# Two expert stages with their tokens sorted by expert on the chip, in units of 128 rows

## The reference, cut to what matters

```python
logits = x @ router.T (+ router_b)          # 8 experts
p = softmax(logits); top_p, top_i = top_k(p, 2)
h = gelu(x @ w1[e].T + b1[e])               # 128 -> 512, e in top_i
y = h @ w2[e].T + b2[e]                     # 512 -> 128
out = sum(top_p * y)                        # block 2: weights scaled to sum 1, and a shared expert for all tokens added
```

## Time and profile before

| | us |
|---|---|
| median of 3 runs (4932.38 to 4941.92) | 4935.69 |
| the profiled execution | 4945.66 |
| its span, first to last instruction | 4943.9 |
| PE busy in it | 3746.8 (76%) |
| DVE, ACT, POOL busy in it | 2553.2, 2187.2, 1043.4 |
| mean granted clock of TensorE | 0.851 of full speed |

### The profile page before, as it was taken

How to read it: one execution, slowest core, us unless ns; L and a number is a source line. 1 busy time by engine, 2 the same in 40 slices (tenths; PEclk the granted TensorE clock), 3 DMA queues, 4 the chain that set the end, 5 groups by cost and what they waited for, 6 DMA issues and landing times. The chain is left out here.

```text
span 4943.9 us, 64940 instructions
## 1 busy us (share of the span) xinstructions
PE 3746.8 (76%) x19738; PEld 2542.2 (51%) x19800; DVE 2553.2 (52%) x6640; ACT 2187.2 (44%) x4248; POOL 1043.4 (21%) x1066
## 2 busy tenths in 40 slices
...
GB/s 37 67 65 5 9 69 26 39 0 0 0 11 10 18 1 1 0 18 1 1 0 16 1 0 0 0 0 34 1 0 0 5 0 0 0 2 0 18 0 17
DMA packets 45621, 58.54 MB, mean 12 GB/s; under 512 B 14058, under 2 KB 37836, under 8 KB 44588
## 3 DMA queue, kind: packets, MB, share of 16 engines
...
## 5 line engine op out<-in xcount | busy, mean ns | idle before, releaser
L418 PEld LDWEIGHTS bank<-moe_w,moe_hidden 128*128 128x128 f32 x5376 | 626.6, 192 | 78.7 <-issue 76.8
L418 PE MATMUL bank<-moe_w,moe_hidden 128*128 128x128 f32 x5376 | 630.3, 275 | 0.0
L408 PE MATMUL bank<-normed_t,moe_w 128*128 (+1 forms) x1344 | 615.6, 600 | 11.5 <-ACT moe_hidden L470 8.2
L470 ACT ACTIVATE moe_hidden<-bank,moe_b 128x512 f32<-128x512 f32 x544 | 372.8, 687 | 505.8 <-PE bank L408 504.3
L546 DVE SCALAR_TENSOR_TENSOR branch<-bank,moe_weights,branch 128x128 f32<-128x128 f32 x768 | 216.3, 345 | 707.8 <-PE bank L418 703.9
L90 POOL TENSOR_TENSOR branch_norm_shifted<-branch_norm_moments,eps 128x4 f32<-128x4 f32 x64 | 12.7, 198 | 1889.8 <-DVE branch_norm_moments L83 1889.8
L408 PEld LDWEIGHTS bank<-normed_t,moe_w 128*128 128x128 f32 x1344 | 244.9, 193 | 256.0 <-issue 240.0
L1987 POOL TENSOR_TENSOR local_size<-local_size,local_half_powers 128x8 f32<-128x8 f32 x128 | 257.0, 2008 | 203.3 <-DVE local_size L2053 199.2
L1691 PE MATMUL bank<-local_wqkv,local_shifted 128*128 128x512 f32 x384 | 211.2, 644 | 57.0 <-DVEq L2045 24.0
L1496 DVE TENSOR_TENSOR ssm_mixer<-ssm_decay,bank 128x384 f32<-128x384 f32 x256 | 133.2, 552 | 202.8 <-PE bank L1158 179.5
L1308 ACT ACTIVATE ssm_decay<-bank 128x384 f32<-128x384 f32 x256 | 120.3, 489 | 192.4 <-PE bank L1131 147.4
...
## 6 DMA issues: line engine op xcount, KB each, us to landing
rwkv_kept<-rwkv_keep SPq DMA_DIRECT2D x8, 768.0 KB, 11.8
...
moe_w<-in_moe_w_dram SPq DMA_DIRECT2D x2, 2048.0 KB
...
```

Source lines behind the costliest of these rows:

```text
L408: pe.matmul(hbank[n % 4][:], w1[:, e, f * P:(f + 1) * P], source_t[:, bass.ds(i * PN, PN)], start=True, stop=True).then_inc(hidden_up, 1)
L418: last = pe.matmul(obank[e % 2][:, t * P:(t + 1) * P], hid[:, e % 2, f, t * P:(t + 1) * P], w2[:, e, f, :], start=(f == 0), stop=(f == chu ...
L470: act.activation(hid[:, e % 2, f, :], hbank[n % 4][:], ACT.Gelu_apprx_tanh, bias=b1[:, n:n + 1] if bias else 0.0).then_inc(hidden_done, 1)
```

## The change

A new function `sorted_moe` takes the place of `moe_block` for `moe0` and `moe2`. It computes a picked expert's rows only.

- The logits come straight from `normed_t` as weights: one matmul of eight columns for each tile, and one addition or copy on DVE for all. `moe_block`, which stays for `moe3`, gets the same logits; it no longer waits for the expert weights ahead of them.
- DVE finds both picks as masks, PE counts (a matmul with ones and one with a triangle of ones), and fourteen more DVE instructions turn the counts into a row number (slot) for each of a token's two picks. The tokens are handled in two halves of 16 tiles. In each half an expert's rows start at a multiple of 128; 40 units of 128 rows hold them whatever the gate says.
- POOL scatters the rows of `normed` to DRAM by slot, one transfer for each tile and pick (64 in all, 32 a half). For `moe0` SP first writes zeros over that DRAM (ten stores of 512 KB).
- For each of the 80 units: SP loads 128 rows, PE transposes them, ACT copies them to `rows_t`, DVE reads the unit's expert number into a register and copies that expert's record (both weight matrices and biases, 1156 numbers a partition) to one of four buffers, PE multiplies up and ACT applies Gelu, PE multiplies down, DVE adds the bias, SP stores 128 rows to DRAM.
- POOL gathers a pair's rows by slot (16 tiles' picks are 32 transfers for four pairs), DVE weighs and adds both picks of a token (`mix`), and the tail follows. The pairs of the first half are mixed in groups 6 to 9 of ten (eight units are a group), those of the second half behind the last unit.
- `moe0`'s shared expert is computed for all pairs ahead of the units, beside the sort.
- `Tail` of the stages ahead of both (`rwkv`, `ssm`) now keeps rows.

PE before: the body of `moe0` for one pair, from the loop's start (names as in the code, without numbers).

The diff, cut to its core:

```diff
--- before.py
+++ after.py
...
         @block.tensor
         def _(pe):
+            pe.wait_ge(router_in, 16 * router_loads)
+            for t in range(TILES):
+                last = pe.matmul(small[:, t * EXPERTS:(t + 1) * EXPERTS], source_t[:, t * P:(t + 1) * P], router[:],
+                                 start=True, stop=True)
+            last.then_inc(logits_up, 1)
...
-                    pe.wait_ge(logits_down, m * 2)
-                    for t in range(PT):
-                        last = pe.matmul(obank[k][:, t * EXPERTS:(t + 1) * EXPERTS],
-                                         logit_rows[:, k, t * P:(t + 1) * P],
-                                         core.ident[0:EXPERTS, 0:EXPERTS], start=True, stop=True)
-                    last.then_inc(logits_up, 1)
...
+UNIT = P
+HALVES = 2
+HALF_TILES = TILES // HALVES
+UNITS = HALF_TILES * 2 + 8
+GROUP = 8
...
+            if shared:
+                sp.wait_ge(blank_ready, 1)
+                for h in range(HALVES):
+                    for g in range(GROUPS_PER_HALF):
+                        sp.dma_start(core.rows_dram[h][g * GROUP * P:(g + 1) * GROUP * P, :].rearrange(
+                            "(k p) c -> p k c", p=P), blank).then_inc(blanked, 16)
+            sp.dma_start(records[:], dram[f"{name}_records"]).then_inc(records_in, 16)
...
+                wait_from(sp, rows_turned, n - GROUP + 1)
+                sp.dma_start(rows_in[:, k, :], core.rows_dram[h][bass.ds(row, P), :]).then_inc(rows_loaded[k], 16)
...
+            def store(h, g, k):
+                n = g * GROUP + k
+                row = (n - h * UNITS) * P
+                sp.wait_ge(out_ready, n + 1)
+                sp.dma_start(core.outs_dram[h][bass.ds(row, P), :], outs[:, k % 4, :]).then_inc(outs_stored[k % 4], 16)
...
+                for k in range(GROUP):
+                    if h + 1 < HALVES and k == 2:
+                        sp.wait_ge(sorted_in[h + 1], 16 * 2 * HALF_TILES)
+                    if k < 2 or h + 1 < HALVES:
+                        load(h + (k >= 2), final_group, k + 6)
+                    store(h, final_group, k)
...
+            def ranks():
+                pe.wait_ge(tables_in, 16)
+                pe.wait_ge(picks_ready, 1)
+                flat = picked[:].rearrange("p t e -> p (t e)")
+                pe.matmul(rbank[:, 0:TILES * EXPERTS], tables[:, ONES:ONES + P], flat, start=True, stop=True)
+                pe.matmul(lbank[:, 0:TILES * EXPERTS], tables[:, EARLIER:EARLIER + P], flat, start=True,
+                          stop=True).then_inc(ranks_up, 1)
...
+            def turn(g, k):
+                g, k = g + k // GROUP, k % GROUP
+                n = g * GROUP + k
+                pe.wait_ge(rows_loaded[k], (g + 1) * 16)
+
+                wait_from(pe, rows_taken, n - 1)
+                pe.transpose(tbank[k % 2][:, 0:UNIT], rows_in[:, k, :], core.ident[:]).then_inc(rows_turned, 1)
+
+            def up(g, k):
+                n = g * GROUP + k
+                pe.wait_ge(rows_taken, n + 1)
+                pe.wait_ge(record_ready, n + 1)
+
+                wait_from(pe, hid_done, n - 1)
+                for f in range(CH):
+                    last = pe.matmul(hbank[k % 2][:, f * UNIT:(f + 1) * UNIT], record[:, k % 4, f * P:(f + 1) * P],
+                                     rows_t[:, k % 2, :], start=True, stop=True)
+                last.then_inc(up_done, 1)
+
+            def down(g, k):
+                g, k = (g, k) if k >= 0 else (g - 1, GROUP - 1)
+                n = g * GROUP + k
+                pe.wait_ge(hid_done, n + 1)
+
+                wait_from(pe, out_ready, n - 1)
+                for f in range(CH):
+                    last = pe.matmul(obank[k % 2][:, 0:C], hid[:, k % 2, f, :],
+                                     record[:, k % 4, W2 + f * P:W2 + (f + 1) * P], start=(f == 0), stop=(f == CH - 1))
+                last.then_inc(down_done, 1)
+
+            def slot(g, k, low=0):
+                final = low == ALL_GROUPS
+                if not (final and k == GROUP - 1):
+                    turn(g, k + 1)
...
+                if not (low == 0 and k == 0):
+                    down(g, k - 1)
...
+                act.activation(rows_t[:, k % 2, :], tbank[k % 2][:, 0:UNIT], ACT.Identity).then_inc(rows_taken, 1)
+
+            def slot(g, k, low=0):
+                n = g * GROUP + k
+                final = low == ALL_GROUPS
+                if not (final and k == GROUP - 1):
+                    take_rows(g, k + 1)
+                act.wait_ge(up_done, n + 1)
+
+                wait_from(act, down_done, n - 1)
+                for f in range(CH):
+                    last = act.activation(hid[:, k % 2, f, :], hbank[k % 2][:, f * UNIT:(f + 1) * UNIT],
+                                          ACT.Gelu_apprx_tanh, bias=record[:, k % 4, B1 + f:B1 + f + 1])
+                last.then_inc(hid_done, 1)
+                if tail.turned and k == 1 and low >= GROUPS_PER_HALF + 2:
...
+            pool.wait_ge(slots_ready, 1)
+            if shared:
+                pool.wait_ge(blanked, 16 * ALL_GROUPS)
+            for t in range(TILES):
+                for k in range(2):
+                    pool.indirect_dma_start(core.rows_dram[t // HALF_TILES][:, :], bass.IndirectOffsetOnAxis(ap=slots[:, k, t:t + 1], axis=0),
+                                            core.normed[:, t, :], None).then_inc(sorted_in[t // HALF_TILES], 16)
+
+            def gather(i):
+                for t in range(i * PT, (i + 1) * PT):
+                    for k in range(2):
+                        pool.indirect_dma_start(found[:, k, t, :], None, core.outs_dram[t // HALF_TILES][:, :],
+                                                bass.IndirectOffsetOnAxis(ap=slots[:, k, t:t + 1], axis=0)
+                                                ).then_inc(found_in[i], 16)
+
+            per_half = PAIRS // HALVES
+            for h in range(HALVES):
+                for b in range(4):
+                    pool.wait_ge(outs_stored[b], 16 * (h + 1) * UNITS // 4)
+                for i in range(h * per_half, (h + 1) * per_half):
+                    gather(i)
+                    if i > h * per_half:
+                        tail.pool(pool, i - 1)
+                tail.pool(pool, (h + 1) * per_half - 1)
+
...
+            each = [P, HE, UNITS]
+            steps = tables[:, STEPS:STEPS + UNITS]
+            dve.scalar_tensor_tensor(wide[:], steps.unsqueeze(1).broadcast_to(each), float(UNIT),
+                                     many[:].unsqueeze(2).broadcast_to(each), ALU.mult, ALU.is_lt)
+            dve.drain()
...
+            flat_both = lambda buffer: buffer[:].rearrange("p k t e -> p k (t e)")
+            by_pick = lambda buffer: buffer[:].rearrange("p k t e -> p (k t) e")
...
+            def fetch(g, k):
+                g, k = g + k // GROUP, k % GROUP
+                n = g * GROUP + k
+                expert = dve.value_load(table[0:1, bass.ds(n, 1)], min_val=0, max_val=EXPERTS - 1)
+
+                wait_from(dve, down_done, n - 3)
+                dve.tensor_copy(record[:, k % 4, :], records[:, bass.ds(expert, 1), :].rearrange(
+                    "p e r -> p (e r)")).then_inc(record_ready, 1)
+
+            def mix(i):
+                dve.wait_ge(found_in[i], 16 * 2 * PT)
...
+                                             share_of[:, 1, i * PT + t:i * PT + t + 1], core.branch[:, t, :],
+                                             ALU.mult, ALU.add)
+                dve.drain()
+                tail.dve_branch(dve, i)
+
+            def slot(g, k, low=0):
...
+                n = g * GROUP + k
+                final = low == ALL_GROUPS
+                if not (final and k + 2 >= GROUP):
+                    fetch(g, k + 2)
+                dve.wait_ge(down_done, n + 1)
+                if not (low == 0 and k < 4):
+                    dve.wait_ge(outs_stored[k % 4], (g * 2 + k // 4) * 16)
+                dve.tensor_tensor(outs[:, k % 4, :], obank[k % 2][:, 0:C], record[:, k % 4, B2:B2 + C],
+                                  ALU.add).then_inc(out_ready, 1)
+                dve.drain()
+
+            fetch(0, 0)
+            fetch(0, 1)
+            groups(dve, slot, ((1, GROUPS_PER_HALF + 1),))
+            for g in range(GROUPS_PER_HALF + 1, ALL_GROUPS):
+                i = g - GROUPS_PER_HALF - 1
+                for k in range(GROUP):
+                    slot(g, k, ALL_GROUPS if g == ALL_GROUPS - 1 else g)
+                    if k == 0:
+                        mix(i)
+                    if k == 3:
+                        tail.dve_stream(dve, i)
+                    if k == 6:
+                        tail.dve_fresh(dve, i)
+            for i in range(PAIRS // 2, PAIRS):
+                mix(i)
...
         if "rwkv" in blocks:
-            rwkv_block(core, Tail(core, "rwkv", keep_rows=False, turned=True), dram["x"])
+            rwkv_block(core, Tail(core, "rwkv", keep_rows=True, turned=True), dram["x"])
             core.end_of_block()
```

(5 more changed lines are left out.)

368 lines of the change are left out of this document (324 added, 44 removed).

## The result

| | us | ratio to before, 95% |
|---|---|---|
| before, in the group of the record | 4936.88 (4932.38 to 4941.92, 4 runs) | |
| changed, on record | 4755.36 (4754.10 to 4758.67, 4 runs) | 0.9633, 0.9616 to 0.965 |
| forecast | 4560 (4450 to 4765) | 0.924 |
| changed again (e9, 2 runs) | 4618.37 | 0.9348, 0.9321 to 0.9375 |
| changed again (e16b, 4 runs) | 4613.50 | 0.9335, 0.9319 to 0.935 |

The kernel is faster, by 182 us where 376 were forecast.

A forecast was written before the change was run, and what follows sets the result against it. PE bound both expert bodies; afterwards DVE was to pace units at 2.25 us. Stages of 369 and 364 us (-216, -149) and -11 in the third gave -376: 4570, or 4560 us on the median's scale, range 4450 to 4765.

The forecast's parts named there:

- The shared expert ends on PE at 14.2 + 60 = 74: First stage's preparation: shared expert at 7.5 us a pair hides the scatter; table load and records follow, first unit at 81.
- C: Dear transfers by row number on POOL: c = 2.2 us each, +151, 4711 us; chance 0.15.
- F: Slower: POOL becomes the bound; with c = 4.5 a stage takes 647 us, in all +184, 5120 us; chance 0.05.
- G: DVE's record copies hold up POOL's transfers, c 1.85 while units run, 9 us a stage: 4578 us; chance 0.04.
- D: A unit's steps don't overlap, since the register read waits until DVE is empty: 3.5 us a unit, +200, 4760; chance 0.12.
- E: TensorE clock granted at 1.2 GHz in the units: 3.86 us a unit on PE, +190, 4750 us; chance 0.06.
- issue price c: POOL's time to issue one scatter or gather by row number: 1.2 us, the middle of 0.33 and 2.2.
- the register read: DVE reading a unit's expert number from SBUF into a register: 1.0 us, the middle of 0.07 and 1.8.
- A: The main case: DVE sets the unit's pace at 2.25 us against PE's 1.93 and ACT's 1.78; 4560 us, chance 0.38.
- B: Cheap register reads at 0.07 us: DVE 1.32 a unit, PE binds at 1.93, 45 less a stage, 4470; chance 0.18.
- PE's busy time: Sign of the forecast: PE busy near 210 us in the first sorted stage and 150 in the second.
- Behind the last unit: Stage ends: POOL's 32 x 1.2 issues, landing, waits and last mix take 73 us, 77 in the second stage.

The follow-up runs named there:

- e9: The changed kernel itself, unaltered, run once more in a later group on chip 4: 4618.37 us (2 runs).
- e16b: The changed kernel itself, unaltered, run beside e15b on chip 2: 4613.50 us (4 runs).
- e7: Changed kernel without the register read: DVE copies the record of expert k for a group's k-th unit, so units meet the wrong expert: 4574.65 us.
- e15b: e13 plus second half's scatter and first half's gathers spread over units, first-stage scatter spaced by small powers, epsilon added by DVE: 4599.81 us (4 runs).
- e11: Changed kernel with the shared expert's pairs 2 to 7 in a loop on PE and ACT, the same file as e4 run again: 4611.30 us.
- e13: Changed kernel with shared expert's bias in DVE's addition, its pairs in loops, POOL's powers between gathers, one register read for two units: 4700.25 us (4 runs).
- e2: Changed kernel with the scatters of both stages replaced by as many plain 64 KB transfers from POOL, rows in order: 4631.65 us.
- e14: Changed kernel with second half's scatter and first half's gathers spread, one behind each of 32 units, and POOL's powers between these gathers: 4647.57 us (2 runs).
- e4: Changed kernel with the shared expert's pairs 2 to 7 in a loop of two pairs on PE and ACT: 4750.86 us.

## Why the forecast was wrong, step by step

**The step that failed** is "The shared expert ends on PE at 14.2 + 60 = 74 ... up to c = 1.3 the scatter costs nothing here", and its twin, units beside transfers at 2.25. On record the shared expert ended at 165.3, and 16 gathers stretched their group from 17 to 34.6 us. What I had wrong is that an engine which issues transfers costs only its own time. Rivals C and F priced POOL's time, G what DVE's copies do to POOL; none had PE, ACT and DVE losing 1.1 us a transfer. It is worth 95 + 48 = 143 us of the 195 by which the result missed (137 to 142 by the medians), and it was absent in four of seven groups of runs, where the miss is 55.

Three things were luck. 4755 lies inside 4450 to 4765, but the upper bound stood for D and E, at 4760 and 4750, and neither came true. The issue price c and the register read, 1.2 and 1.0, were middles between rows of other kinds. Measured are 1.27 (0.96 busy and 0.30 between), and for the read some 0.8: the gap ahead of a record copy is 0.98 in the mean with it and 0.16 without it, in e7.

**The rest, against e16b.** First stage 401.7 for 369, second 378.7 for 364, third 274.9 for 270.7.
- First unit: PE's first matmul of one at 101.6 us (972.38) for 81. The logits were right (13.8 for 12), the sort and gate ready at 39 for 34, hidden. The shared expert was mis-sized: I charged 7.5 us a pair with its bias matmuls, it takes 9.4.

```profile
940.50 3.60 PE L693 MATMUL bank<-normed_t,moe_own 128*128 128x512 f32 x8
944.03 0.48 PE L702 MATMUL bank<-moe_own,ones_row 1*128 1x128 f32 x2
944.45 1.16 PE L704 MATMUL bank<-moe_own,moe_found 128*128 128x128 f32 x8
```

  A bias product with one row takes 0.41 (944.03 to 944.45), a full one of 128 columns 0.27 (four in some 1.09, to the next bias). Four of the first are 1.65 a pair where I had charged 0.49, and sixteen of the second 4.4 where rows 3 gave 3.57: over eight pairs 16 of the 20.6 us. Both come with the one-row products: in e15b, without them, 32 full ones take 7.31 us, 0.23 each, and the shared expert ends at 75.2, where I had 74; with its loop alone (e11) it ends at 94.8.
- Second stage's first unit at 77.4 for 72: slots at 31.8 for 29, 32 issues in 40.8 for 38.
- Units: 218 and 217 us from the first matmul to the last addition, for 214. A unit 2.13 (forecast 2.25), a group with a pair 27.8 and 27.3 (26.4). The gap ahead of the record copy is 0.91 to 1.27 (1.0 taken, and 0.15 for drains), the copy 0.76 (0.80), the addition 0.29 (0.30), in e16b's timeline:

```profile
1060.42 0.29 DVE L1008 TENSOR_TENSOR moe_outs<-bank,moe_record 128x128 f32<-128x128 f32 x1 [0.35 <-PE bank L748]
1061.98 0.76 DVE L979 COPY moe_record<-moe_records 128x1156 f32 x1 [1.27 <-issue]
1062.66 0.28 DVE L1008 TENSOR_TENSOR moe_outs<-bank,moe_record 128x128 f32<-128x128 f32 x1
```

  So A's account of the unit stands, and e7 shows both its halves: without the read 1.90, for 1.93. The rival B's 0.07 is out, D too. The floor of about 600 ns for a tensor_load in the Trainium skill ("DMA: Bandwidth & Descriptors", "Latency and other measured facts") is below these gaps, which contain the read and a drain, and below the some 0.8 of the read alone.
- PE's busy time, a sign of the forecast at near 210 and 150, was 279 and 195 in e16b. In the first stage the shared expert with its ranks is 79 of it, for 60, the first 48 units are 104, for 93 at 1.93 each, and the other 32, at a clock of 0.85, 78, for 62.
- Behind the last unit: 82 and 84, for 74 and 78 with the barrier's 1.4. Most of what is missing is a drain of POOL between two small operations, where gathers stand just ahead of them. In e16b's timeline:

```profile
1231.39 0.21 POOL L92 TENSOR_TENSOR branch_norm_shifted<-branch_norm_moments,eps 128x4 f32<-128x4 f32 x1
1233.37 1.04 POOL L94 TENSOR_TENSOR branch_norm_rstd<-branch_norm_shifted,minus_half 128x4 f32<-128x4 f32 x1 [1.77 <-issue]
...
1237.80 0.20 POOL L92 TENSOR_TENSOR x_norm_shifted<-x_norm_moments,eps 128x4 f32<-128x4 f32 x1 [3.40 <-DVE x_norm_moments L85]
1238.15 1.01 POOL L94 TENSOR_TENSOR x_norm_rstd<-x_norm_shifted,minus_half 128x4 f32<-128x4 f32 x1
```

  1.77 us behind gathers, 0.15 where none came since the last drain. Three pairs have it once. A pair takes 17.9 us (1204.80 to 1222.68), and I had 8 x 1.2 + 6 = 15.6. e13 keeps the drains and ends at 77 in both stages, e15b has none and ends at 70 and 74. Transfers in flight can't be all of it: on record the first such gap of a stage's units is 6.71 us, at 1172.6, 18 us behind the last gather, where e16b's gathers land in 2.5. What the drain waits for is open.
- Third stage: its 64 matmuls took 13.8, at the lower clock (0.50 granted), for 12, and the gain was 6.9 for 11.

**The other rivals.** E: no unit took the 3.86 us of the lower clock. Over the first 40 units it is 0.98 and 0.97 in the two stages of e16b, in groups 6 to 9 0.85 and 0.86; whether that has a part in the 0.9 to 1.4 us that a group takes over the forecast is not separated. In the held-up stretch on record it is 0.89 in 911 to 938, where PE begins to starve at 928, and 0.50 behind it. G: sixteen gathers beside record copies stand 1.38 apart (1063.2 to 1083.9 in e16b), against 1.26 without: 0.12 each, not 0.65, and it costs nothing. What I had excluded without a row is that one engine's transfers could hold up the instructions of another; the trace of before had no transfer of this kind, and my rivals on transfers were all within POOL.

**What stays open.** Why the hold-up came in three groups (the record, chip 5, once chip 2) and not in four (chips 2 twice, 4, 8), and by which path. Against lack of DMA throughput stands e2. A supply that runs dry would fit the 18 us until it begins, "issue" in front of instructions without a wait, three engines at once, and e14; but against late code stands e4, whose loop ran 373 matmuls without a packet of PE's code and was held up all the same. The Trainium skill ("Runtime: NRT & Kernel Launch", "Instruction fetch mechanics") has the sequencers fetch blocks of 256 instructions by their own DMA queue, mostly hidden. The traces agree on the size: q8's packets have 16 KB, one for some 130 matmuls and as many loads. Both instruction queues moved the same at both levels (64 and 93 packets), and a block that comes late should stop PE at the end of the one before, not let one instruction through per 2.8 us (an argument; no run delays a block). So the slow step lies behind that queue, and no run shows which it is. Every execution here was recorded by the profiler; whether the hold-up comes without it is not shown either.
